# Dealing the second layer norm of a scan kernel between GpSimd and ScalarE, block by block

## The reference, cut to what matters

```
d, B, C = x @ x_proj_w.T            # 128 + 16 + 16 columns
delta   = softplus(d @ dt_proj_w.T + dt_proj_b)
h[t]    = exp(delta[t] * A) * h[t-1] + delta[t] * B[t] * x[t]   # 16 states a channel
y[t]    = sum_n C[t] * h[t] + x[t] * D
x1      = layernorm(x + y)
v       = (x1 @ weight) * scale
v       = v * tanh(|v|)/(|v| + eps), clipped to norm 0.99
out     = layernorm(x1 + v)
```

## Time and profile before

| | |
|---|---|
| median of 3 runs | 1258.63 us (1256.66 to 1259.16) |
| profiled execution: its own time | 1252.72 us |
| profiled execution: span of the slowest core | 1251.1 us (eight cores: 1243.5 to 1251.1) |
| busy share of the span: DVE, ACT, POOL, PE | 93%, 79%, 77%, 76% |

### The profile page before, as it was taken

The page is one execution under the profiler, slowest core; times in us unless marked ns, Lnnn a source line. Parts: engine busy times, 40 slices in busy tenths (PEclk is TensorE's granted clock), DMA queues, the critical chain, the costliest instruction groups (busy, mean ns, idle before and its releaser), DMA issues.

```text
span 1251.1 us, 28397 instructions; the slowest of 8 cores (1243.5 to 1251.1 us)
## 1 busy us (share of the span) xinstructions
PE 946.6 (76%) x8913; PEld 589.9 (47%) x8913; DVE 1161.3 (93%) x613; ACT 988.3 (79%) x1711; POOL 960.7 (77%) x658
## 2 busy tenths in 40 slices
PE   4466666776688997667679898577669998887892
PEld 1344444454455655444445555344445555544541
DVE  1899999999999999999999899999999999998845
ACT  1667776677778799999877699999977798998835
POOL 2986767667997666788998567788998676689872
PEclk9588888888899998978899999988799999998996
DMA  7398669755759976434639974544667976467795
GB/s 112 94 140 145 134 114 142 117 120 98 134 81 199 189 156 73 63 95 107 147 84 168 171 174 89 77 87 106 127 110 139 181 143 127 91 131 167 138 165 172
DMA packets 337184, 159.67 MB, mean 128 GB/s; under 512 B 311280, under 2 KB 320592, under 8 KB 335248
## 3 DMA queue, kind: packets, MB, share of 16 engines
q1 hardware_dynamic: 326256, 134.27, 56.4%
q0 software_dynamic: 10784, 23.60, 11.8%
HBM read 83.29 MB, written 25.23 MB: 87 GB/s over the span
## 4 chain that ended last, share of the span: by engine, by line
DVE 26%; ACT 25%; issue 22%; PE 9%; SPq 7%; POOL 6%; DMA 3%; ACTq 1%; DVEq 0%; POOLq 0%
DVE h L1546 25%; ACT dae_x L1180 11%; ACT dae_x L1178 7%; POOL g L633 3%; PE pa L878 2%; SPq L487 2%; SPq L442 2%; DMA x_b<-xT 2%; PE pb L947 1%; POOL r_b L737 1%; DMA w_sl<-wbf 1%; SPq L415 1%; PE pa L1040 1%; ACT delta L1161 1%; ACT r_b L1216 1%
## 5 line engine op out<-in xcount | busy, mean ns | idle before, releaser
L1546 DVE TENSOR_TENSOR_SCAN h<-dae_x,pa 128x1024 bf16<-128x1024 f32 x512 | 1120.7, 2263 | 29.8 <-PE pa L878 20.6
L633 POOL TENSOR_TENSOR g<-h,C_rep 128x1024 bf16<-128x1024 bf16 x320 | 677.9, 2126 | 207.9 <-DVE h L1546 198.5
L878 PE MATMUL pa<-diagB,uT 128*128 128x128 bf16 x4096 | 369.4, 234 | 227.7 <-DVE h L1546 216.2
L1178 ACT ACTIVATE dae_x<-delta,c_A 128x512 f32<-128x512 bf16 x512 | 367.0, 717 | 181.2 <-DVE h L1546 179.9
L878 PEld LDWEIGHTS pa<-diagB,uT 128*128 128x128 bf16 x4096 | 276.1, 104 | 408.6 <-issue 388.6
L1180 ACT ACTIVATE dae_x<-delta,c_A 128x511 f32<-128x511 bf16 x512 | 361.6, 706 | 0.0
L947 PE MATMUL pb<-r_b,w_sl 128*128 128x512 bf16 x768 | 198.4, 380 | 9.1 <-DMA w_sl<-wbf 9.1
L838 PE MATMUL pb<-g,eye_b 128*128 128x512 bf16 x320 | 137.3, 429 | 18.8 <-ACT r_b L1216 14.2
L840 PE MATMUL pb<-g,eye_b 128*128 128x512 bf16 x320 | 135.5, 424 | 0.0
L857 PE MATMUL pb<-diagC,hT 128*128 128x128 bf16 x1536 | 128.2, 231 | 1.2 <-DMA hT<-h 1.2
L857 PEld LDWEIGHTS pb<-diagC,hT 128*128 128x128 bf16 x1536 | 106.8, 105 | 21.9 <-issue 10.4
(11 more groups left out here) (181 smaller groups left out, 728.6 us busy)
## 6 DMA issues: line engine op xcount, KB each, us to landing
w_sl<-wbf SPq DMA_DIRECT2D x64, 512.0 KB, 4.3
wbf<-wsw POOLq DMA_DIRECT2D x16, 512.0 KB, 6.7
out<-r_b SPq DMA_DIRECT2D x8, 1024.0 KB, 4.5
x_b<-xT POOLq DMA_DIRECT2D x15, 512.0 KB, 10.2
C_rep<-bcscr SPq DMA_DIRECT2D x20, 256.0 KB, 5.3
out<-r_b POOLq DMA_DIRECT2D x4, 1024.0 KB, 6.1
hT<-h SPq DMA_TRANSPOSE x192, 3.7
out<-diagB SPq DMA_DIRECT2D x4, 512.0 KB, 4.8
```

The lines of the kernel that those rows point to most:

```text
L633: e.tensor_tensor(s.g[:, g % NG, :, :], s.h[:, p, :, :], s.C_rep[:, GP.index(p), :, :], ALU.mult).then_inc(S["cmul"], 1)
L878: mm = e.matmul(s.ps_b[:, k % 2, n, tb * 128:(tb + 1) * 128], s.uT[:, j % 3, tb, :], s.diagB[:, p, tb, n, :], start=True, stop=True, skip_ ...
L1178: e.activation(s.dae_x[:, k % 3, 0, :], s.delta[:, j % 3, :], AF.Exp, scale=s.c_A[:, n:n + 1])
L1546: e.tensor_tensor_scan(s.h[:, p, :, :].rearrange("p n t -> p (n t)"), s.dae_x[:, k % 3, :, :].rearrange("p n t -> p (n t)"), s.ps_b[:, k % ...
```

## The change

In all three rounds blocks 0 and 2 are normed and stored by POOL, blocks 1 and 3 normed by ACT and stored by SP. The squares move from +3 to +4, the small operations from +4 to +5, the norm from +5 to +6 on either engine, and SP's store from +6 to +7. The starts of the blocks, the scaling (+0) and the add (+1) stay. Waits on "stored" name the semaphore of the engine that stored the block before.

```diff
+def norm_on_pool(tb):
+    return tb % 2 == 0
+
+def stored(n):
+    return "out_p" if norm_on_pool(n % NTB) else "out_st", (n // 2 + 1) * 16
...
     def sync_program(s, e):
-            if r2_at(k, 6) and c < LAST:
-                s.sync_out(e, *r2_at(k, 6))
+            hit = r2_at(k, 7)
+            if hit and not norm_on_pool(hit[1]):
+                s.sync_out(e, *hit)
...
     def gpsimd_program(s, e):
-            hit = r2_at(k, 5)
-            if hit and hit[0] == LAST - 1:
-                s.gpsimd_norm(e, hit[1])
+            hit = r2_at(k, 6)
+            if hit and norm_on_pool(hit[1]):
+                s.gpsimd_norm(e, *hit)
...
     def gpsimd_r2(s, e, c, tb):
-        if c == LAST - 1 and tb > 0:
-            e.wait_ge(S["out_p"], tb * 16)
-        elif n > 0:
-            e.wait_ge(S["out_st"], n * 16)
+        if n > 0:
+            e.wait_ge(S[stored(n - 1)[0]], stored(n - 1)[1])
...
     def scalar_r2(s, e, k):
-        if r2_at(k, 3):
-            s.scalar_r2sq(e, *r2_at(k, 3))
-        if r2_at(k, 4):
-            c, tb = r2_at(k, 4)
+        if r2_at(k, 4):
+            s.scalar_r2sq(e, *r2_at(k, 4))
+        if r2_at(k, 5):
+            c, tb = r2_at(k, 5)
...
-        hit = r2_at(k, 5)
-        if hit and hit[0] < LAST - 1:
+        hit = r2_at(k, 6)
+        if hit and not norm_on_pool(hit[1]):
```

More of the change, by code:

```diff
@@ L400, in sync_program @@
                         in_=s.r2_late[tb][:, col]).then_inc(S["out_st"], 16)
-        e.wait_ge(S["out_p"], NTB * 16)
-        e.wait_ge(S["out_st"], (LAST - 1 + 2) * NTB * 16)
+        e.wait_ge(S["out_p"], LAST * NTB // 2 * 16)
+        e.wait_ge(S["out_st"], (LAST * NTB // 2 + 2 * NTB) * 16)
     def sync_tokens(s, e, c, st):
@@ L431, in sync_out @@
         row = c * TL + tb * 128
-        e.wait_ge(S["o_ev"], c * NTB + tb + 1)
+        e.wait_ge(S["o_ev"], (c * NTB + tb) // 2 + 1)
         e.dma_start(out=s.out_d[row:row + 128, :], in_=s.r2_b[:]
@@ L744, in gpsimd_r2, with gpsimd_norm @@
         s.token_mean(e, c, tb)
-    def gpsimd_norm(s, e, tb):
+    def gpsimd_norm(s, e, c, tb):
         S = s.sem
@@ L749, in gpsimd_norm @@
         col = slice(tb, tb + 1)
-        e.wait_ge(S["nmr"], n_a2(LAST - 1, tb))
+        e.wait_ge(S["nmr"], n_a2(c, tb))
         e.tensor_scalar(s.r2_b[:], s.r2_b[:], t("rq")[:, col],
@@ L753, in gpsimd_norm @@
                         ).then_inc(S["o_ev_p"], 1)
-        row = (LAST - 1) * TL + tb * 128
-        e.wait_ge(S["o_ev_p"], tb + 1)
+        row = c * TL + tb * 128
+        e.wait_ge(S["o_ev_p"], (c * NTB + tb) // 2 + 1)
         e.dma_start(out=s.out_d[row:row + 128, :], in_=s.r2_b[:]
@@ L1254, in scalar_srr @@
             e.wait_ge(S["rt_in"], (c + 1) * NDT * 16)
[L1255 to L1258, removed]
             if c > 0:
+                e.wait_ge(S[stored(c * NTB - 1)[0]], stored(c * NTB - 1)[1])
                 e.wait_ge(S["row"], n_row(c - 1, "var"))
```

## The result

The change made the kernel slower by half a per cent: ratio 1.0049, 95% interval 1.0038 to 1.0061, from twenty runs of each on one chip (medians 1261.03 us after, 1254.62 before; the 1258.63 that the prediction started from was the median of three runs). The prediction was no change, +0.4 us; measured is +6.2 (0.0049 x 1254.6). The 1259.0 comes within 2.0 of the measured 1261.03, and 1261.03 falls inside the stated range of 1253.8 to 1264.0, by luck: the sum started 4 us too high. The same range around 1254.62 would be 1249.8 to 1260.0, and the measured time lies above that. It is the difference that has to be explained.

A forecast was written before the change was run, and what follows sets the result against it. POOL's arrival at the add of block 3 was taken to set the round's end. On 1252.7, +3.0 for two rounds and -2.6 for the third gave 1253.1; the runs' median, 5.9 higher, made it 1259.0 us; range 1253.8 to 1264.0.

The forecast's parts named there:

- What bounds the rounds: First two rounds: POOL's arrival at the add of block 3 sets the end; DVE's wait there grows to 2 to 3 us.
- ACT was the bound and POOL has room: Rival, first two rounds: the multiplies' slack swallows POOL's later work, 2.6 us gained each; 1250.8 us in all, chance 0.10.
- The price of a norm on POOL: On POOL, the next multiply starts 3.3 us after a norm, counting its wait and the store's issue.
- It lands by about 549.1, taking 6.5 ... no wait: First round: block 0's store lands in 6.5 us, just before the add of block 1, which waits for nothing.
- ACT's wait before the square of block 1: First two rounds: ACT waits about 1.2 us for the add of block 1 before squaring it.
- Block 2's landing: First two rounds: block 2's store lands in 6.5 us and holds the add of block 3, 1.5 us later than before.
- stores of POOL become the wait: Rival, first two rounds: block 2's store lands after 9 us, each round loses 2.5 us more; 1264 us, chance 0.25.
- landings outside 5.6 to 9.5: Sign of being wrong: any of POOL's stores landing in less than 5.6 or more than 9.5 us.
- First two rounds together: Two rounds at +1.5 us each, +3.0 in all; bounds a round -0.3 and +4.5.
- The second rival: Landings at 5.6 us in each round: first two +0.6 each, third -4.2; 1255.6 us, chance 0.20.
- The third round's inside: Third round: POOL loses two norms, ACT gains two; last scan 2.6 us earlier, between -4.2 and -0.3 by the landing.
- What follows the last scan is not touched: End of the kernel: the stretch behind the last scan stays as it was, a difference of 0.

The follow-up runs named there:

- e4: The changed kernel with all blocks stored by SP, POOL only norming; ratio 0.9966 to the kernel before.
- e5: The changed kernel with only block 0's store of every round moved from POOL's queue to SP's; ratio 0.9997 to the kernel before.
- e9: e4 with block 3 of the third round normed and stored by POOL; ratio 0.9971 to the kernel before.
- e10: e9 without the delay of one step in the third round; ratio 0.9973 to the kernel before.
- e7: The changed kernel's deal of norms and stores without the delay of one step, in all rounds; ratio 1.0057 to the kernel before.

## What the prediction had right and what it had wrong

No change was forecast and a loss of half a per cent was measured, a case to which the prediction gave a chance of 0.28. What bounds the rounds and what a norm costs came out as argued; two steps failed, the landing of block 0's store and the end of the kernel.

- **What bounds the rounds: right.** The argument was that POOL's arrival at the add of block 3 sets the round's end. From that add to scan 264 it is 40.39 to 40.48 us in all fourteen kernels and on every core, whether the round took 61.9 or 66.5 us. DVE waits for POOL there for 0.28 + 1.65 = 1.9 us, 0.63 before; 2 to 3 was predicted. The rival "ACT was the bound and POOL has room" fell with it.
- **The price of a norm on POOL, 3.3 us: right.** 2.05 for the norm and 1.3 for the store (e4 against e5).
- **"It lands by about 549.1, taking 6.5 ... no wait": the step that failed in the first two rounds.** The landing of block 0's store took 8.7 us on the mean, not 6.5, and the add of block 1 waited for it, 1.4 us on the core shown and 1.9 on the mean. I took the middle of POOL's four landings and discounted the one of 9.5 as one beside weight loads. What stood 0.25 us ahead of that one, in the third round of before, was a `uT` transpose. These are the rows of SP's queue and of POOL that I should have read side by side:

```profile
1162.88 1.19 SPq L478 DMA_TRANSPOSE uT<-u_b  x1
```
```profile
1163.13 0.62 POOL L756 DMA_DIRECT2D out<-r_b  x1 [0.56 <-POOL r_b L751]
```

  Those rows alone could not have told the two causes apart: in the kernel before the two loads of that step stand just ahead of the same `uT`. On five cores loads and transpose were ahead of the store, which took 8.3 to 9.7 us; on three they were 0.4 us and more behind it, and it took 6.0 to 6.5. In the first round of the changed kernel no load is near, and an `hT` stands 0.14 to 0.16 us ahead of block 0's store on all eight cores.
- **ACT's wait before the square of block 1: 2.63 to 4.0 us, not 1.2.** It follows from that landing: 2.63 less the 1.37 that the add itself waited is 1.26. The scaling of block 2 came later, and the gap ahead of its add was 1.45, predicted 1.2.
- **Block 2's landing: too slow.** I had 6.5 and a wait; it took 4.4 to 4.5, and no add waited. From the add of block 2 to that of block 3 it is 22.3 us, predicted 22.9; from block 0's to block 1's it is 24.0 on the core shown and 24.5 on the mean, predicted 22.5. So block 2 gave back 0.6 of the 1.5 to 2.0 us that block 0 cost. The rival "stores of POOL become the wait" named this block; it was right about the mechanism and wrong about the block. Its threshold was off as well: the sum passes +2.5 from a landing of 7.6 us on, not 7.8. And "landings outside 5.6 to 9.5" was a sign of being wrong, which came true: 4.4. The Trainium skill's price (DMA: Bandwidth & Descriptors, section "Anatomy of one DMA"), an estimate of 4.4 us for 1 MB issued by GpSimd, holds for this store, and not for block 0's 8.7. SP's stores, which that section does not speak of, took 4.3 to 4.7 in the first round.
- **First two rounds together: +5.4, predicted +3.0.** Each round (+3.05 and +2.36) stays under the bound of +4.5, but that bound was meant for block 2's landing, and the loss came from the block that was thought safe.
- **The second rival's sum was off.** It books landings at 5.6 us as +0.6 a round, but by the prediction's own steps POOL is free for the add of block 3 only at 591.3, which is +1.0. It would have given 1256.4, not 1255.6.
- **The third round's inside: right.** Lost from 473 to 511: 7.32 to 5.01, -2.3, predicted -2.6. The waits around scans 488 to 490 fell from 4.4 to 3.2, predicted 2.7.
- **"What follows the last scan is not touched": the second step that failed.** The last `hT` was issued at 90.0 us, where it had been at 89.9: the scans ended 2.3 earlier and SP did not. I had looked at what waits for SP's store and not at what else the queue holds at that time. The stretch after the last scan grew by 3.1, and the end came 0.8 later, not 2.6 earlier. Of the 3.1, 2.5 are `hT` falling behind scan 509 (1.9 to 4.3 us after its end); the other 0.7 come after `hT` is issued and have no cause shown.
- **The sum.** Predicted 3.0 - 2.6 = +0.4; measured 5.4 - 2.3 + 3.1 = +6.2. Of the miss of 5.8, 2.4 are the first two rounds, 0.3 the third round's inside and 3.1 the end.

What stays open: why a store that POOL issues right behind a DMA transpose is slow together with it (only that they are, and that a lead of 1.9 us or SP as the issuer avoids it). Also the last microsecond of the end: from DVE's first addition of a token block behind the last scan (`r_b<-eT,tok,rT`) to the end it takes 16.1 us in e5, 16.2 in before and 18.2 in e9 and e10, and no run tells why.

## What to carry to other kernels

A store costs twice: the engine that issues it spends the issue and the wait for its data, and what needs the buffer waits for the landing, which depends on what other queues issue in that microsecond. When work is dealt between two engines, move the arithmetic and leave the stores with the queue that has nothing else to compute; here that alone was worth 0.8%. And where a stretch ends earlier, look for the first queue that does not: its order was written for the old times, and it keeps them.

## What was not expected of the hardware

In the first round a GpSimd store of 1 MB lands in 4.4 to 4.7 us with no transpose close to it (block 2 after the change, block 0 in e7), and in 8.2 to 9.6 when it is issued 0.14 to 0.16 us behind a DMA transpose of SyncE's. Over all profiles it is 5.7 to 11.3 with the transpose up to 0.35 us ahead, and 4.7 to 6.5 with it up to 0.3 behind. The transposes suffer as well: the `hT` took 8.6 and the `uT` 7.5 us to land, where with the store out 1.9 us ahead (e7) they took 4.0 and 2.8. SyncE's own store, 0.5 us ahead of the same transpose (e4), landed in 4.4 to 4.6, the transposes in 5.2 and 3.3.
